# A third buffer for whole tiles, and three multiplies on GpSimd in place of two, in a three-layer graph network kernel

## What is computed

```
h = relu(layernorm(x))
for i in 0, 1, 2:
    W   = (edge_attr @ edge_w[i] + edge_b[i]).reshape(E, 16, 16)
    msg = einsum('ei,eio->eo', h[src], W)
    h   = segment_sum(msg, dst, num_segments=12500) + h @ root_w[i] + root_b[i]
    if i < 2: h = batchnorm(h) * gamma[i] + beta[i]
    h = relu(h)
out = x + h @ pred_w + pred_b
```

## Time and profile before

| | us |
|---|---|
| median of 3 runs | 9503.38 |
| fastest, slowest | 9480.78, 9513.57 |
| the profiled execution | 9474.14 |
| its span on the core | 9472.3 |
| busy in it: PE | 8251.2 (87%) |
| DVE | 7729.4 (82%) |
| ACT | 6611.7 (70%) |
| POOL | 6060.3 (64%) |

### The profile page before, as it was taken

One profiled execution on the slowest core, in us unless ns is written; L12 is line 12 of the kernel. 1 busy time (PEld: TensorE's weight loads), 2 busy tenths in 40 slices (PEclk: granted clock), 3 DMA queues, 4 the chain that ended last, 5 costly groups with the idle time before them and its releaser, 6 DMA issues. The chain is left out here.

```text
span 9472.3 us, 130730 instructions
## 1 busy us (share of the span) xinstructions
PE 8251.2 (87%) x45302; PEld 7735.4 (82%) x45302; DVE 7729.4 (82%) x9298; ACT 6611.7 (70%) x10329; POOL 6060.3 (64%) x6355
## 2 busy tenths in 40 slices
PE   6888888888888788888888888888888888888887
PEld 4888888888888588888888888868888888888887
DVE  6888888888888788888888888878888888888886
ACT  5767777677677677676777767767776777777775
POOL 3666666666666456666666666645666666666664
PEclk8999999999999799999999999979999999999998
DMA  3111111111111111111111111111111111111110
GB/s 38 24 24 25 23 25 25 25 24 23 24 25 25 20 24 25 24 25 23 24 25 23 24 24 25 25 21 23 24 25 24 24 25 25 24 24 23 24 25 18
DMA packets 485264, 228.89 MB, mean 24 GB/s; under 512 B 345853, under 2 KB 435853, under 8 KB 484603
## 3 DMA queue, kind: packets, MB, share of 16 engines
q1 hardware_dynamic: 271316, 172.14, 7.2%
q0 software_dynamic: 180000, 46.44, 5.9%
q10 hardware_dynamic: 33287, 1.92, 0.4%
HBM read 216.52 MB, written 3.52 MB: 23 GB/s over the span
## 5 line engine op out<-in xcount | busy, mean ns | idle before, releaser
L1117 PE MATMUL bank<-nodes,low_hot 128*128 128x400 f32 x30000 | 5985.4, 356 | 1099.3 <-DVE spread L680 969.6
L1117 PEld LDWEIGHTS bank<-nodes,low_hot 128*128 128x128 f32 x30000 | 5558.6, 194 | 1371.9 <-DVE spread L680 1077.8
L487 POOL DMA_INDIRECT xg<-node_table,idx x5625 | 5399.2, 960 | 1840.8 <-issue 1543.1
L944 ACT ACTIVATE distance<-key_all,low_id 128x640 bf16<-128x640 int16 x3000 | 2235.3, 815 | 1174.7 <-PE bank L1117 885.8
L680 DVE TENSOR_TENSOR spread<-mask,bank 128x400 f32<-128x400 uint8 x3750 | 2024.4, 565 | 381.1 <-PE bank L1117 302.3
L948 ACT ACTIVATE low_hot<-distance,one 128x640 fp32r<-128x640 bf16 x3000 | 2229.0, 813 | 0.0
L687 DVE TENSOR_REDUCE xg<-spread 128x80 f32<-128x2000 f32 x750 | 1677.1, 2236 | 25.6
L467 POOL TENSOR_TENSOR xbig<-xg,ea 128x384 f32<-128x384 f32 x720 | 660.3, 917 | 1485.0 <-DMA xg<-node_table,idx 1019.8
L725 DVE TENSOR_TENSOR xparts<-xbig,bank 128x504 fp32r<-128x504 f32 x1500 | 1019.0, 679 | 637.7 <-ACT bank L905 537.5
L905 ACT ACTIVATE bank<-cut_room 128x504 f32<-128x504 f32 x1500 | 887.7, 592 | 840.7 <-issue 431.9
L627 DVE TENSOR_TENSOR hot<-bank,dst_rel 128x2800 fp32r<-128x2800 f32 x375 | 1149.0, 3064 | 0.0
(11 more groups left out here) (108 smaller groups left out, 1872.3 us busy)
## 6 DMA issues: line engine op xcount, KB each, us to landing
key_all<-edge_keys SPq DMA_DIRECT2D x375, 320.0 KB
xg<-node_table,idx POOLq DMA_INDIRECT x5625
ea<-in_edge_attr SPq DMA_DIRECT2D x375, 60.0 KB
ea<-in_edge_attr SPq DMA_DIRECT2D x375, 40.0 KB
idx<-in_src SPq DMA_DIRECT2D x375, 7.5 KB
node_table<-rows SPq DMA_DIRECT2D x3, 781.2 KB
...
```

The lines of the kernel that those rows point to most:

```text
L487: pool.indirect_dma_start(out=xg[u][:, j, :], out_offset=None, in_=table[:, :], in_offset=bass.IndirectOffsetOnAxis(ap=idx[u][:, j:j + 1], ...
L944: nc.scalar.activation(distance[f][:, 0:tiles.stop - tiles.start, :], key[u % KEYS][:, tiles, :], ACT.Abs, bias=low_id[:, f:f + 1]).then_i ...
L1117: last = nc.tensor.matmul(p_sel[t % BANKS], low_hot[:, f, t, :], nodes[i][:, f, :, :].rearrange("p d f -> p (d f)"), start=(f, i) == (0, 1 ...
```

## The change

There are now 13 split and 12 whole tiles, with the split tiles last. A third buffer for whole tiles lies in the memory of `rows`, which is used only between layers. POOL multiplies tiles 0 to 2 and 3 to 5 ahead of gathers 6 and 11 of their slot, and tiles 6 to 8 ahead of gather 1 of the next slot. Each of these batches has its own semaphore, so a multiply waits for its own three gathers and no later ones, and for the sum of slot k-3 in place of k-2. DVE multiplies the other three whole tiles. In the first 20, 10 and 10 slots of the three layers (`LEAD`) DVE multiplies all twelve, and POOL waits at three places a slot until all gathers issued so far have landed.

```diff
 PAIR = 2
-CUT = 14
+CUT = 13
 ROUNDS = 4
 QUAD = 4
 PARTS = (slice(0, 5), slice(5, 10))
 HALF = 5
 KEYS = 3
 TURNS = 3
-RESTS = (5, 12)
-EARLY = 6
-LEAD = SLOTS
+BATCH = 3
+BATCHES = 3
+RESTS = {1: 2, 6: 0, 11: 1}
+LEAD = (20, 10, 10)
+TRIPLE = 3
 WIN = 112
 NODE_P = 125
 ROOM = 4
...
-        SPLIT = slice(EARLY, EARLY + CUT)
-        LATE = slice(EARLY + CUT, TILES)
-        EACH = EARLY // len(RESTS)
-        assert EARLY == EACH * len(RESTS) and all(EACH * (i + 1) <= r for i, r in enumerate(RESTS))
-        assert FETCHED <= SPLIT.stop <= FETCHED + PARTS[0].stop
+        WHOLE, SPLIT = slice(0, TILES - CUT), slice(TILES - CUT, TILES)
+        EARLY = BATCHES * BATCH
+        LATE = slice(EARLY, TILES - CUT)
+        assert EARLY <= WHOLE.stop <= FETCHED
         assert CUTS % ROUNDS == 0 and ROUND <= 512
         xbig = sb("xbig", [P, CUTS + PAIR * WHOLES])
         xs = xbig[:, 0:CUTS].rearrange("p (a b) -> p a b", b=WIDTH)
+        row_room = sb("row_room", [P, max(WHOLES, PER * D)])
+        rows = row_room[0:NODE_P, 0:PER * D].rearrange("p (m d) -> p m d", d=D)
         xw = [xbig[:, CUTS + i * WHOLES:CUTS + (i + 1) * WHOLES].rearrange("p (a b) -> p a b", b=WIDTH)
               for i in range(PAIR)]
+        xw.append(row_room[:, 0:WHOLES].rearrange("p (a b) -> p a b", b=WIDTH))
         x_far = xbig[:, 0:CUTS + WHOLES].rearrange("p (a b) -> p a b", b=WIDTH)
         hot = [sb(f"hot{i}", [P, TILES, WIN], F32R) for i in range(PAIR)]
 
 
-        cut_room = sb("cut_room", [P, CUTS])
-        xcut = cut_room[:]
...
+        def batch_of(j, u):
+
+            return s_batch[j // BATCH][u] if j < EARLY else s_gath[u]
+
+        def land_first(eng, body, u, count):
+
+            for i in range(BATCHES):
+                some = min(BATCH, max(0, count - i * BATCH))
+                if body * BATCH + some:
+                    eng.wait_ge(s_batch[i][u], (body * BATCH + some) * 16)
+            if body * LATER + max(0, count - EARLY):
+                eng.wait_ge(s_gath[u], (body * LATER + max(0, count - EARLY)) * 16)
+
         def early_to(layer, g):
-            return len(RESTS) * (layer * (G - LEAD) + max(0, g - LEAD + 1))
+            return BATCHES * (sum(G - n for n in LEAD[:layer]) + max(0, g - LEAD[layer] + 1))
...
-            def multiply_early(layer, b, u, i):
-
-                k = layer * G + b * SLOTS + u
-                here = slice(i * EACH, (i + 1) * EACH)
-                pool.wait_ge(s_seg, k + CREDIT - 1)
-                nc.gpsimd.tensor_tensor(
-                    xw[k % PAIR][:, here, D:D + FD].rearrange("p j (f d) -> p j f d", d=D),
-                    xg[u][:, here, :].unsqueeze(2).to_broadcast([P, EACH, F, D]),
-                    ea[u][:, here, :].unsqueeze(3).to_broadcast([P, EACH, F, D]), ALU.mult).then_inc(s_early, 1)
+            def multiply(layer, g, i):
+
+                if g >= LEAD[layer]:
+                    k = layer * G + g
+                    u = g % SLOTS
+                    here = slice(i * BATCH, (i + 1) * BATCH)
+                    pool.wait_ge(s_batch[i][u], (layer * BODIES + g // SLOTS + 1) * 16 * BATCH)
+                    pool.wait_ge(s_seg, k + CREDIT - 2)
+                    nc.gpsimd.tensor_tensor(
+                        xw[k % TRIPLE][:, here, D:D + FD].rearrange("p j (f d) -> p j f d", d=D),
+                        xg[u][:, here, :].unsqueeze(2).to_broadcast([P, BATCH, F, D]),
+                        ea[u][:, here, :].unsqueeze(3).to_broadcast([P, BATCH, F, D]), ALU.mult).then_inc(s_early, 1)
 
             def gather(layer):
...
                         for j in range(FETCHED):
                             if j in RESTS:
-                                pool.wait_ge(s_gath[u], (layer * BODIES + b) * (16 * FETCHED) + 16 * j)
-                                if b * SLOTS + u >= LEAD:
-                                    multiply_early(layer, b, u, RESTS.index(j))
+                                multiply(layer, b * SLOTS + u - (RESTS[j] == BATCHES - 1), RESTS[j])
+                                if b * SLOTS + u < LEAD[layer]:
+                                    land_first(pool, layer * BODIES + b, u, j)
                             pool.indirect_dma_start(
                                 out=xg[u][:, j, :], out_offset=None, in_=table[:, :],
                                 in_offset=bass.IndirectOffsetOnAxis(ap=idx[u][:, j:j + 1], axis=0),
-                            ).then_inc(s_gath[u], 16)
+                            ).then_inc(batch_of(j, u), 16)
+                multiply(layer, G - 1, BATCHES - 1)
                 far = farthest(pool)
                 with pool.If(far > WIN - 1):
                     gather_far(layer)
...
-                dve.wait_ge(s_gath[u], body * (16 * FETCHED) + 16 * FETCHED)
-                dve.wait_ge(s_xg, k * 2 + 1)
+                dve.wait_ge(s_gath[u], (body + 1) * 16 * LATER)
+                dve.wait_ge(s_xg, k * 2 + 2)
...
             def multiply_whole(layer, b, u):
 
                 k = layer * G + b * SLOTS + u
-                dve.wait_ge(s_xg, k * 2 + 2)
-                dve.wait_ge(s_seg, k + CREDIT - 1)
-                if b * SLOTS + u < LEAD:
-                    products(xw[k % PAIR][:, 0:EARLY, :], xg[u][:, 0:EARLY, :], p_ea[k % PAIR][:, 0:EARLY, :])
-                products(xw[k % PAIR][:, EARLY:, :], xg[u][:, LATE, :], p_ea[k % PAIR][:, LATE, :]).then_inc(s_prod, 1)
+                body = layer * BODIES + b
+                dve.wait_ge(s_gath[u], (body + 1) * 16 * LATER)
+                dve.wait_ge(s_seg, k + CREDIT - 2)
+                if b * SLOTS + u < LEAD[layer]:
+                    for i in range(BATCHES):
+                        dve.wait_ge(s_batch[i][u], (body + 1) * 16 * BATCH)
+                    products(xw[k % TRIPLE], xg[u][:, WHOLE, :], p_ea[k % PAIR][:, WHOLE, :]).then_inc(s_prod, 1)
+                else:
+                    products(xw[k % TRIPLE][:, LATE, :], xg[u][:, LATE, :],
+                             p_ea[k % PAIR][:, LATE, :]).then_inc(s_prod, 1)
...
-                act.wait_ge(s_gath[u], (layer * BODIES + b) * (16 * FETCHED) + 16 * FETCHED)
-                act.wait_ge(s_xg, k * 2 + 1)
+                act.wait_ge(s_gath[u], (layer * BODIES + b + 1) * 16 * LATER)
+                act.wait_ge(s_xg, k * 2 + 2)
...
             def copy_other_rows(layer, b, u):
 
                 k = layer * G + b * SLOTS + u
-                act.wait_ge(s_xg, k * 2 + 2)
-                act.wait_ge(s_seg, k + CREDIT - 1)
-                nc.scalar.activation(xw[k % PAIR][:, 0:EARLY, 0:D], xg[u][:, 0:EARLY, :], ACT.Copy)
-                nc.scalar.activation(xw[k % PAIR][:, EARLY:, 0:D], xg[u][:, LATE, :], ACT.Copy).then_inc(s_xc, 1)
+                for i in range(BATCHES):
+                    act.wait_ge(s_batch[i][u], (layer * BODIES + b + 1) * 16 * BATCH)
+                act.wait_ge(s_gath[u], (layer * BODIES + b + 1) * 16 * LATER)
+                act.wait_ge(s_seg, k + CREDIT - 2)
+                nc.scalar.activation(xw[k % TRIPLE][:, :, 0:D], xg[u][:, WHOLE, :], ACT.Copy).then_inc(s_xc, 1)
 
...
-                split = range(SPLIT.start, SPLIT.stop)
-                whole = (*range(EARLY), *range(LATE.start, TILES))
-                for j in (*split[:-1], *whole, split[-1]):
-                    ends = dict(start=j == split[0], stop=j == split[-1])
-                    if j in split:
-                        last = nc.tensor.matmul(p_parts, onehots[:, j, :],
-                                                xparts[:, :, j - EARLY, :], **ends)
+                first, last = SPLIT.start, TILES - 1
+                for j in (*range(first, last), *range(first), last):
+                    ends = dict(start=j == first, stop=j == last)
+                    if j >= first:
+                        done = nc.tensor.matmul(p_parts, onehots[:, j, :],
+                                                xparts[:, :, j - first, :], **ends)
                     else:
-                        nc.tensor.matmul(p_z, onehots[:, j, :].bitcast(F32), wholes[:, whole.index(j), :], **ends)
-                return last
+                        nc.tensor.matmul(p_z, onehots[:, j, :].bitcast(F32), wholes[:, j, :], **ends)
+                return done
 
             def sum_tiles_far(products, onehots):
...
-                        if b * SLOTS + u >= LEAD:
+                        if b * SLOTS + u >= LEAD[layer]:
...
-                        sum_tiles(xw[k % PAIR], hot[k % PAIR]).then_inc(s_seg, 1)
+                        sum_tiles(xw[k % TRIPLE], hot[k % PAIR]).then_inc(s_seg, 1)
```

26 lines of the change are left out of this document (14 added, 12 removed).

## The result

The changed kernel takes 9247.3 us (median of three runs, 9243.0 to 9252.3) beside 9495.6 us for the kernel before on the same chip. The ratio is 0.9738, with a 95% interval from 0.9714 to 0.9762: 2.6% faster, 248 us. I had forecast 9398 us and a range from 9280 to 9500. (A fourth run, at a granted clock of 0.23, is left out.)

What follows compares the result with a forecast made beforehand. The prediction took a loop through ACT, DVE and PE as the bound. It summed 0.24 us in 289 slots and 0.42 in 86 to 105 us, giving a 9398 us median, range 9280 to 9500.

Steps and rivals of the forecast that it cites:

- POOL is in none of its steps: The loop that sets the slot's pace runs through ACT, DVE and PE, 23.78 us, without POOL.
- their removal is worth nothing by itself: POOL's landing waits, 1019.8 us in all, are spare time; removing them only makes room for the third multiply.
- What PE's records show of the sum's length, 4.7 us, is too little: PE's sum ahead of L896: it lasts 8.3 us for the engines that wait for it.
- the dear case of 0.44: Twelfth whole tile in PE's sum: it lengthens the sum by 0.44 us if whole tiles cause all that records miss.
- the term of 0.20 us: Twelve whole tiles in PE's sum: sum 0.20 us longer per slot, taken between 0 and 0.44.
- the second rival: The twelfth whole tile costs waiters nothing: 168 us gained, 9335 us; also stands for a warmer clock; chance 0.28.
- The split tile: 13 split tiles for 14: L901 saves 0.12 us and the four ACT and DVE rounds 0.27, together 0.39 a slot.
- L716 was to lose 0.08 us: DVE's L716 loses a fourteenth of 1.21 us, counting only in the 86 slots where it comes last.
- The one copy for L967 and L968: ACT's single copy between L896 and L901: 0.05 us gained where the sum comes last.
- first, second and fourth rival: First split matmul to L896's counterpart: 8.5 as forecast (0.46), 8.3 whole tile free (0.28), 8.8 whole tile dear (0.13).
- The third rival: POOL's multiplies hold up L716 through shared SBUF ports, 0.42 us a slot: 53 us slower, 9556 us; chance 0.09.
- The fifth rival: POOL becomes the pace if batches land late, 25.6 us a slot with the old waits: 9970 us; chance 0.04.

Runs made afterwards that it cites:

- e11: Kernel before with 13 split and 12 whole tiles, also keeping the new tile order, one copy and batch semaphores: 9352 us, ratio 0.9988.
- e6: Kernel before with only 12 of a slot's 15 gathers issued from the second five slots of each layer on: 9328 us, ratio 0.9971.
- e15: Kernel before with 13 split and 12 whole tiles and only 12 of 15 gathers a slot, old buffers, multiplies and landing waits: 9070 us, ratio 0.9549.
- e17: Test kernel computing nothing of the reference, stages of sums and picks beside gathers, VectorE work and loads: 1702.8 us, against 1461.8 on another chip.
- e1: Kernel after with two buffers, two multiplies and all landing waits as before, keeping 13 split tiles: 9598 us, 1.0075 of the kernel before.
- e9: Kernel before, unchanged, run again for its trace on another chip: 9362 us, ratio 1.0002.
- e10: Kernel after, unchanged, run again beside the kernel before on another chip: 9065 us, 0.9683 of the kernel before.
- e7: Kernel after with its landing waits in all slots instead of the first of each layer: 10344 us, 1.106 of the kernel before.

## Why the forecast was wrong, point by point

**The step that failed** is the one on GpSimd. "POOL is in none of its steps", and its landing waits are spare time, so that "their removal is worth nothing by itself": that held only for waits that the profile names. On the chip of the result GpSimd's gathers put 0.65 us a slot between the cut's end and ACT's next copy, by a late count of the sum. The forecast read this wait as the sum's own length, kept it and made it 0.20 us longer; in after it is 0.03 us. On the second kind of chip, without the change, the loop of fifteen gathers, two multiplies and two landing waits is 23.88 us against 23.78 for ACT, DVE and PE; a second bound, 0.1 us behind the first, takes all that is saved in the first (e11). I had this number, 24.55 us in the earlier trace rows beside a slot of 24.19, and put it aside because nobody waited for gathers. On the first kind they did wait, for PE.

**The late count.** "What PE's records show of the sum's length, 4.7 us, is too little" had the wrong cause. The sum takes 5.15 us (e6, e15); the other 3 us in before came with the gathers. That PE itself is held up in them, although its records of the sum in before run at the full rate, is argued from after and e17, where the records show it. I wrote that I would be wrong most of all if that wait followed something else in the slot than the number of tiles, and it does: e1 and e15 have the same tiles, and three fewer gathers take the count from 3.66 to 0.01 us late. The twelfth whole tile costs what the records said. In slots in which the granted clock stays at 1.00 through the sum, its records last 4.71 us in e6 and e9 and 4.82 in e10, e11 and e15, 0.11 to 0.12 us more, and the dear case of 0.44 is out. But in after the cut came last in all 288 slots, so the term of 0.20 us counted nothing; in this effect the second rival, with 0.28, was right.

**The split tile.** 0.39 us was right for what it counted: one-hots start 0.38 or 0.39 us earlier after ACT's copy in every pair of the table. What it left out lies between the seventh and the last take: 2.63 us in e6, 2.38 in e15. There PE waits for a bank and then makes the last pick. Picks of e9, then of e10:

```profile
L1117 PE MATMUL bank<-nodes,low_hot 128*128 128x400 f32 x30000 | 5992.5, 357 | 981.2 <-DVE spread L680 955.1 <-DVE nodes L648 15.9 <-DVE agg L592 1.5
```

```profile
L1144 PE MATMUL bank<-nodes,low_hot 128*128 128x400 f32 x30000 | 5929.3, 355 | 802.0 <-DVE spread L702 784.4 <-DVE nodes L670 15.8 <-DVE agg L614 1.4
```

The wait fell from 955 to 784 us, and the mean granted clock rose from 0.925 to 0.942 over the span. I had put the clock into the second rival without a price. The traces give it one. The last pick, eight matmuls after that wait, takes 1.8 us by its records where the granted clock is 1.00 (2.4 GHz) and 2.9 us where it is 0.50 (1.2 GHz). In e6 it ran at the lower level in 168 of the 288 slots, in e15 in 109: 59 slots at 1.16 us are 0.24 us a slot, nearly the whole difference between 2.63 and 2.38, and over half of the 0.39 itself. From e9 to e10 it is 147 and 114 slots. That the shorter wait before it is what keeps the clock up was not tested.

**L716 and the copy.** L716 was to lose 0.08 us; it went from 1227 to 1221 ns in after, and from 1233 to 1189 in e10. The one copy for L967 and L968 shows where the sum came last: from L896 to L901 it is 0.52 us in before and 0.44 from one counterpart to the other in e1, 0.08 us where I took 0.05. In after the sum came last in no slot of the table, so this term counted nothing either. I had left the cut last in 86 slots; it was last in 362.

**The sum of the terms.** From before to after a slot lost 0.63 us in the table, where I had 0.28. It was not made of my terms: the time from ACT's copy to the cut's end is the same (23.53 and 23.52), for the 0.38 us that the one-hots start earlier were lost again to picks held up in their turn (last take 6.33 us after the one-hots, 5.92 before; it comes 0.52 us after the end of the last pick's records, 0.04 in before). What went is the 0.65 us between the cut's end and the next copy, the wait for the late count. In after GpSimd has five gathers between two multiplies and reaches the sum at another point of them; 73% of the counts are late there, and the mean over all is 1.1 us instead of 2.8. That it is the shorter row which brings the count forward fits e15, where three gathers fewer leave rows of seven and five, but no run changes the rows alone. So the sign of the forecast is owed in part to luck: on this chip the gain came from the wait that I had expected to grow.

**The signs.** The rounds are 1.27 or 1.28 us apart and L928 takes 1.78 us, as forecast. The slot is 23.68 us instead of 23.9, L923 is idle for 54.8 us instead of over 457, and the count comes 6.4 us after the first split matmul; I had said 8.5, 8.3 or 8.8 for the first, second and fourth rival.

**GpSimd in after** needs about the 21.7 us that I had added up (21.5 a slot by the steps between its instructions in layer 1, without the waits ahead of multiplies) and waits for PE, 392 us in the two rows above, as forecast. The third rival did not show: multiplies of after take 0.90 us on average, but the cut waits for ACT (424 us), not the other way. **The fifth rival**, GpSimd as the pace with its old waits, is what e7 built: 1.106, where I had 9970 us, 1.049.
